# One fp32r pass less in fc1: w1 split into a power of two and a mantissa, with the scales multiplied into the sums in PSUM

## The reference, cut to what matters

```python
def _dequant(q, scales, g):                      # g = 128
    w = (q.astype(jnp.float32) - 128.0).reshape(K // g, g, N) * scales[:, None, :]
    return w.reshape(K, N)
pooled = ...                                     # scores, masked softmax, weighted sums, for each row
h = (pooled - mu) * rsqrt(var + EPS) * ln_gamma + ln_beta
w1 = _dequant(fc1_q, fc1_scales, 128)            # (512, 2048), scales (4, 2048)
y = silu(h @ w1 + fc1_bias)
w2 = _dequant(fc2_q, fc2_scales, 128)            # (2048, 512)
return x + pooled + 0.5 * (y @ w2 + fc2_bias)
```

## Time and profile before

| | us |
|---|---|
| time, median of three runs | 1589.35 (1588.07 to 1591.4) |
| the profiled execution: its time | 1588.93 |
| the profiled execution: its span | 1587.1 |

### The profile page before, as it was taken

One profiled execution on the slowest core, in us unless ns is written; L12 is line 12 of the kernel. 1 busy time (PEld: TensorE's weight loads), 2 busy tenths in 40 slices (PEclk: granted clock), 3 DMA queues, 4 the chain that ended last, 5 costly groups with the idle time before them and its releaser, 6 DMA issues.

```text
span 1587.1 us, 20994 instructions
## 1 busy us (share of the span) xinstructions
PE 1571.5 (99%) x7259; PEld 1270.1 (80%) x7259; DVE 950.5 (60%) x1918; ACT 432.0 (27%) x662; POOL 177.9 (11%) x156
## 2 busy tenths in 40 slices
PE   8999999999999999999999999999999999999999
PEld 5778788787887878788787887878878787887887
DVE  7887556655665565646666566556655656466522
ACT  3553322222231232312322222222322223123111
POOL 4102011110101101011110111101011010111100
PEclk9999999999999999999999999999999999999999
DMA  9803022040310404013040220403104040130200
GB/s 283 234 1 80 1 47 61 2 105 1 54 55 14 93 1 89 19 26 81 1 107 1 41 66 1 107 1 54 53 12 96 1 84 24 24 83 0 54 1 27
DMA packets 271311, 82.75 MB, mean 52 GB/s; under 512 B 247498, under 2 KB 248036, under 8 KB 270692
## 3 DMA queue, kind: packets, MB, share of 16 engines
q1 hardware_dynamic: 271152, 81.31, 21.7%
q10 hardware_dynamic: 52, 0.01, 0.0%
HBM read 49.83 MB, written 16.78 MB: 42 GB/s over the span
## 4 chain that ended last, share of the span: by engine, by line
PE 95%; DVE 3%; ACT 1%; issue 1%; DMA 0%; SPq 0%; DVEq 0%; ACTq 0%
PE y_ps L1045 14%; PE z_ps L1079 14%; PE z_ps L1080 14%; PE z_ps L1081 14%; PE y_ps L1046 14%; PE y_ps L1047 14%; PE a_ps L1009 1%; PE a_ps L1014 1%; PE a_ps L1010 1%; PE a_ps L1011 1%; PE a_ps L960 1%; PE a_ps L962 1%; PE a_ps L961 1%; PE a_ps L966 1%; PE a_ps L977 1%
## 5 line engine op out<-in xcount | busy, mean ns | idle before, releaser
L561 ACT ACTIVATE y_f<-y_ps,vec_cols 128x512 f32<-128x512 f32 x256 | 176.6, 690 | 912.7 <-PE y_ps L1047 901.8
L1045 PE MATMUL y_ps<-hT_hi,w_hi 128*128 128x512 f32 x1016 | 406.4, 400 | 0.3
L1079 PE MATMUL z_ps<-w_hi,y_hi 128*128 128x512 f32 x1024 | 398.7, 389 | 0.1
L1081 PE MATMUL z_ps<-w_hi,y_lo 128*128 128x512 f32 x1024 | 398.4, 389 | 0.0
L1080 PE MATMUL z_ps<-w_lo,y_hi 128*128 128x512 f32 x1024 | 398.4, 389 | 0.0
L1046 PE MATMUL y_ps<-hT_lo,w_hi 128*128 128x512 f32 x1016 | 396.7, 390 | 0.0
L1047 PE MATMUL y_ps<-hT_hi,w_lo 128*128 128x512 f32 x1016 | 396.6, 390 | 0.0
L849 DVE CAST y_hi<-y_f 128x512 fp32r<-128x512 f32 x240 | 109.6, 457 | 248.8 <-PE z_ps L1081 204.0
L1045 PEld LDWEIGHTS y_ps<-hT_hi,w_hi 128*128 128x128 f32 x1016 | 191.1, 188 | 60.2 <-issue 21.1
L1046 PEld LDWEIGHTS y_ps<-hT_lo,w_hi 128*128 128x128 f32 x1016 | 191.0, 188 | 42.1 <-issue 3.6
L1079 PEld LDWEIGHTS z_ps<-w_hi,y_hi 128*128 128x128 f32 x1024 | 192.2, 188 | 40.4 <-DVE w_lo L840 0.5
(11 more groups left out here) (208 smaller groups left out, 1199.8 us busy)
## 6 DMA issues: line engine op xcount, KB each, us to landing
x<-in_x_dram SPq DMA_DIRECT2D x64, 256.0 KB, 3.4
out_dram<-x SPq DMA_DIRECT2D x64, 256.0 KB, 2.2
x_cols<-in_x_dram SPq DMA_DIRECT2D x240, 64.0 KB, 2.2
h_cols<-scratch SPq DMA_DIRECT2D x224, 64.0 KB, 2.1
fc_codes<-in_L_ffn_fc_q_dram SPq DMA_DIRECT2D x8, 1024.0 KB, 15.2
fc_scaled<-in_L_ffn_fc_scales_dram SPq DMA_DIRECT2D x8, 1024.0 KB, 17.0
scratch<-in_L_cond_W_dram SPq DMA_DIRECT2D x1, 256.0 KB, 4.7
b2h<-in_L_ffn_fc_bias_dram SPq DMA_DIRECT2D x1, 256.0 KB, 15.4
```

Source lines behind the costliest of these rows:

```text
L561: nc.scalar.activation(y_f[k % 2][:], y_ps[k % 2][:], ACT.Silu, bias=b1[:, k:k + 1]).then_inc(silu_done, 1)
L1045: mm(o, w1_hi[:, c, cols], hT_hi[:, c, :], start=(c == 0), stop=False)
L1079: mm(z_ps[r][:], y_hi[k % 2][:, rows], w2_hi[:, k, :], start=(k == 0), stop=False)
L1081: last = mm(z_ps[r][:], y_lo[k % 2][:, rows], w2_hi[:, k, :], start=False, stop=(k == NF - 1))
```

## The change

w1 is kept as (code - 128) x 2^e, where e is the exponent of the scale. Such a value has at most 8 bits, so fp32r holds it exactly and there is no low part: `fc1` has two matmuls for each row block (w1 x hT_hi, w1 x hT_lo). The mantissas m of the scales, per output column, which is a PSUM partition, are applied to the sums. After row block c the sum is multiplied by m[c] / m[c + 1] (`ratio`), in place in PSUM, and Silu's own scale is m[3]. The multiplication (`rescale`) is ScalarE's for even k and VectorE's for odd k. TensorE's next matmul on that bank waits for it.

To give it time, fc1 works two k at a time, interleaved by c with fc2: an element is 32 slots, and slot i holds fc1(k, c), fc1(k + 1, c) with (k, c) from `fc1_slot(i)`, the conditioner's steps of that slot, and two of the four rows r of fc2(i // 2). So fc1 runs on into the next element from slot 27. The steps of the conditioner have new slots; those with a negative number are worked in slots 28 to 31 of the element before (in element 0 all are 4 later). `finish` is two and two, around slot 31's other steps. h is transposed into a buffer of its own, `h_rows`. SP loads the columns of x for element b + 1 ahead of `move_h(b)`. The exponential is in three pieces on three slots. The third and fourth load of w1's codes wait until the units of the first and second are made, since the scales' buffer is now double. The scales come in a second time, as 64 rows that TensorE transposes with the other vectors; RATIO makes mantissas and ratios of them in the prologue.

```diff
+        PE_PLAN = {-2: [("AT", 0)], -1: [("AT", 1)], 0: [("AT", 2)], 1: [("AT", 3)], 2: [("SC", 0)],
+                   9: [("USUM", 0), ("U", 0)], 11: [("DSUM", 0)], 13: [("PZ", 0)], 14: [("PZ", 1)], 15: [("PZ", 2)],
+                   16: [("PZ", 3)]}
+        ACT_PLAN = {-4: [("XT", 0)], -3: [("XT", 1)], -1: [("XT", 2)], 0: [("XT", 3)], 1: [("TANH", 0)], 2: [("SC", 0)],
+                    7: [("EXPE", 0), ("EXP", 0)], 8: [("EXP", 1)], 9: [("EXP", 2)], 10: [("U", 0)], 13: [("PZ", 0)],
+                    14: [("PZ", 1)], 15: [("PZ", 2)], 16: [("PZ", 3)]}
+        DVE_PLAN = {-4: [("TURN", 0), ("TURN", 1)], -3: [("XT", 0), ("TURN", 2)], -2: [("XT", 1), ("TURN", 3)],
+                    -1: [("XT", 2)], 0: [("XT", 3)], 1: [("PAR", 0)], 3: [("SCAN", 0)], 4: [("COLS", 0)],
+                    5: [("ROWMAX", 0)], 6: [("ARGS", 0)], 7: [("XS", 0)], 10: [("PC", 0), ("USUM", 0)],
+                    11: [("U", 0), ("XS", 1)], 12: [("DSUM", 0)], 14: [("LN", 0), ("XS", 2)],
+                    15: [("LN", 1), ("XS", 3)], 16: [("LN", 2)], 17: [("LN", 3)], 18: [("RSTD", 0)], 19: [("H", 0)]}
...
+        ACT_MOVED = {25: [("AFFINE", 0), ("AFFINE", 1)], 26: [("AFFINE", 2), ("AFFINE", 3)]}
+        DVE_MOVED = {24: [("TURNH", 0), ("TURNH", 1), ("TURNH", 2), ("TURNH", 3)], 26: [("SPLITH", 0), ("SPLITH", 1)],
+                     27: [("SPLITH", 2)], 28: [("SPLITH", 3)]}
...
+        DVE_LATE = {0: [("L2", 1), ("D1", 4)], 1: [("D2", 2)], 3: [("L2", 2)], 4: [("D2", 4)], 5: [("D1", 6)], 6: [("L2", 4)],
+                    8: [("D2", 6)], 9: [("D1", 8)], 10: [("L2", 6)], 12: [("D2", 8)], 13: [("D1", 10)], 14: [("L2", 8)],
+                    16: [("D2", 10)], 17: [("D1", 12)], 18: [("L2", 10)], 19: [("D2", 12)], 22: [("L2", 12)]}
...
+        def fc1_slot(i):
+
+            g, c = divmod(i + 5, ND)
+            return g // NH, 2 * (g % NH), c
...
+                for k0 in w1_unit:
+                    if k0 // NG == g - 2:
+                        sp.wait_ge(w1_unit[k0], 2)
                 load_w1(g)
                 load_w2(g)
...
             def turn(b, p):
 
+                sp.wait_ge(xs_used, (b + 1) * NJ)
+                load_columns(b + 1)
                 if not by_pe(b):
                     move_h(b)
-                sp.wait_ge(xs_used, (b + 1) * NJ)
-                load_columns(b + 1)
...
+            def rescale(b, k, c):
+
+                act.wait_ge(part_done, part_count(b, k, c))
+                nc.scalar.activation(y_ps[k % 2][:], y_ps[k % 2][:], ACT.Copy, scale=ratio[:, c * NF + k:c * NF + k + 1]).then_inc(scaled[0], 1)
...
+            def ffn(b):
+                for i in range(SLOTS):
+                    ahead, k, c = fc1_slot(i)
+                    if not (ahead and is_last(b)):
+                        if c < ND - 1:
+                            rescale(b + ahead, k, c)
+                        else:
+                            silu(b + ahead, k)
+                            silu(b + ahead, k + 1)
+                    if is_first(b) and i % 4 == 0:
+                        y_hi_part(i // 2 + 1)
+                    if is_first(b) and i % 4 == 3 and i < SLOTS - 1:
+                        y_hi_part((i + 1) // 2)
+                    for ahead, name, n in cond_steps(b, i, ACT_PLAN, ACT_TURN, ACT_MOVED):
+                        steps[name](b + ahead, n)
...
+            for c in range(3):
                 h_scaled(0, c)
+            act.wait_ge(ratio_ready, 1)
+            rescale(0, 0, 0)
+            h_scaled(0, 3)
+            for c in (1, 2):
+                rescale(0, 0, c)
+            for t in (0, 1):
+                silu(0, t)
+            y_hi_part(0)
+            for k0 in (0, 1):
+                w2_hi_part(k0)
+            rescale(0, 2, 0)
...
             def w1_values(k0):
+                q, e, w = w1_views(k0)
+                bits = e.bitcast(I32)
+                dve.wait_ge(w1_in[k0 // NG], 32)
+                v.tensor_scalar(bits, bits, 23, 23, ALU.logical_shift_right, ALU.logical_shift_left).then_inc(w1_unit[k0], 1)
+                dve.wait_ge(w1_unit[k0], 1)
+                v.scalar_tensor_tensor(w, q, -128.0, e, ALU.add, ALU.mult).then_inc(w1_unit[k0], 1)
...
+            def rescale(b, k, c):
+
+                dve.wait_ge(part_done, part_count(b, k, c))
+                v.tensor_scalar(y_ps[k % 2][:], y_ps[k % 2][:], ratio[:, c * NF + k:c * NF + k + 1], None, ALU.mult).then_inc(scaled[1], 1)
...
+            def ffn(b, p):
+                chains = {1: Chain(b + 1), 2: Chain(b + 2)}
+                for i in range(SLOTS):
+                    ahead, k, c = fc1_slot(i)
+                    if c < ND - 1 and not (ahead and is_last(b)):
+                        rescale(b + ahead, k + 1, c)
+                    if i % 4 == 0:
+                        split_y(b, i // 2 + 1)
+                    if i % 4 == 3 and i < SLOTS - 1:
+                        split_y(b, (i + 1) // 2)
+                    if i == SLOTS - 1:
+                        if not is_last(b):
+                            split_y(b + 1, 0)
+                        finish(b, p, 0)
+                        finish(b, p, 1)
+                    for ahead, name, n in cond_steps(b, i, DVE_PLAN, DVE_TURN, DVE_MOVED):
+                        steps[name](b + ahead, n, p if ahead == 2 else 1 - p, chains[ahead])
+                    if is_first(b):
+                        for name, k0 in DVE_LATE.get(i, []):
+                            weights[name](k0)
+                finish(b, p, 2)
+                finish(b, p, 3)
...
+            def fc1(b, k, c):
+
+                if c == 0:
+                    if k >= 2 or not is_first(b):
+                        pe.wait_ge(silu_done, b * NF + (k - 1))
+                    if is_first(b) and k in w1_unit:
+                        pe.wait_ge(w1_unit[k], 2)
+                else:
+                    pe.wait_ge(scaled[k % 2], scale_count(b, k, c - 1))
+                if k == 0:
+                    pe.wait_ge(hT_done, b * ND + (c + 1))
+                o, w = y_ps[k % 2][:], w1[:, c, k * P:(k + 1) * P]
+                mm(o, w, hT_hi[:, c, :], start=(c == 0), stop=False, skip_group_check=True)
+                last = mm(o, w, hT_lo[:, c, :], start=False, stop=True, skip_group_check=True)
+                last.then_inc(part_done if c < ND - 1 else fc1_done, 1)
...
+            def ffn(b, p):
+                for i in range(SLOTS):
+                    ahead, k, c = fc1_slot(i)
+                    if not (ahead and is_last(b)):
+                        fc1(b + ahead, k, c)
+                        fc1(b + ahead, k + 1, c)
+                    for ahead, name, n in cond_steps(b, i, PE_PLAN, PE_TURN, {}):
+                        steps[name](b + ahead, n, p if ahead == 2 else 1 - p)
+                    for r in (2 * (i % 2), 2 * (i % 2) + 1):
+                        fc2(b, i // 2, r)
```

More of the change, by code:

```diff
@@ L212, in build @@
         hT_done = sem("hT_done")
+        part_done = sem("part_done")
+        scaled = [sem(f"scaled{i}") for i in range(2)]
+        ratio_ready = sem("ratio_ready")
         fc1_done = sem("fc1_done")
@@ L228, in build @@
[L228 to L233, removed]
+        z_rows = sem("z_rows")
@@ L268, in by_pe, with cond_steps @@
             return isinstance(a, int) and a <= 1
-        def plan(b, early, steady):
-            return early if isinstance(b, int) and b == 0 else steady
+        def cond_steps(b, i, steps, turn, moved):
+            first = isinstance(b, int) and b == 0
+            out = []
+            if not (isinstance(b, int) and b == B - 1):
+                out += [(1, name, n) for name, n in steps.get(i - DELAY if first else i, []) if first or i >= 0]
+                out += [(1, name, n) for name, n in (turn if first else moved).get(i, [])]
+            if not (isinstance(b, int) and b >= B - 2):
+                out += [(2, name, n) for name, n in steps.get(i - SLOTS, [])]
+            return out
@@ L891, in _ @@
                     sum_identities()
+                elif name == "RATIO":
+                    scale_ratios()
                 else:
@@ L1071, in fc2 @@
-            def fc2(b, k):
-                if is_first(b) and k in w2_unit:
-                    pe.wait_ge(w2_unit[k], 3)
-                pe.wait_ge(split_done, b * NF + (k + 1))
-                if k == 0 and not is_first(b):
-                    pe.wait_ge(final_done, b * NJ)
-                for r in range(NJ):
-                    rows = slice(r * P, (r + 1) * P)
-                    mm(z_ps[r][:], y_hi[k % 2][:, rows], w2_hi[:, k, :], start=(k == 0), stop=False)
-                    mm(z_ps[r][:], y_hi[k % 2][:, rows], w2_lo[:, k, :], start=False, stop=False)
-                    last = mm(z_ps[r][:], y_lo[k % 2][:, rows], w2_hi[:, k, :], start=False, stop=(k == NF - 1))
-                    if is_last(b) and k == NF - 1:
-                        last.then_inc(last_rows, 1)
-                if not (is_last(b) and k == NF - 1):
-                    last.then_inc(fc2_done, 1)
```

(15 more changed lines are left out.)

286 lines of the change are left out of this document (110 added, 176 removed), and 7 rows, old and new, of tables (DVE_LATE, DVE_STEADY).

## The result

The changed kernel takes 1622.2 us against 1589.4: a ratio of 1.0197, 95% interval 1.0173 to 1.0222, so it is slower, though the interval doesn't say whether by more or by less than 2%. Ratio and interval rest on two runs, of 1622.2 and 1620.0 us; a third took 2727.1 us at the full clock, for a reason that nothing here shows. The forecast was 1580, faster. The profiled execution has a span of 1620.6 us, 33.5 more than before, at a mean granted clock of TensorE of 0.963, where before had 0.999.

The account below looks back on a forecast made before the run. TensorE, busy for 99% of the span, was taken as the bound. 1587.1 + 10.6 (element 0) + 13 x (96.5 - 96.6) - 4.5 (element 14) - 13.5 (element 15) = 1578.1, with 1.8 outside 1580 us; range 1530 to 1622.

Parts of the forecast that it names:

- What it takes away: In fc1, one of three matmuls goes: 1024 at 0.227 us, 232 us, leaving a period of 82.1 us.
- What it adds: 48 multiplications in PSUM per element, 24 on ScalarE at 0.69 us and 24 on VectorE at 0.75 us.
- rival 1: VectorE's multiplication in PSUM runs at SBUF's rate, 0.49 us, saving about 4 us an element: 1528 us; chance 0.15.
- The loop: In steady slots TensorE waits for multiplications queued behind other work: 14.4 us a period, making it 96.5 us.
- Slot 24's multiplication behind the transposes: On VectorE, rescale 25 queues behind h's transposes, which wait for move_h: TensorE waits 3.6 us.
- XT chain on ScalarE: Around slot 28, XT 0 waits for TURN 0 and ScalarE's rescale 29 stands behind it: 2.1 us.
- slot 31 and its neighbours: split_y, finish steps and XT 2 and 3 delay projections 2 and 3: waits of 1.1 and 0.6 us.
- the slack misses: In slots of 3 modulo 4, split_y precedes the next slot's fc2, leaving 0.09 us slack: 0.8 us added.
- Rival 2: Waits overlap as one long stall empties the queues, so they cost 8 us an element: 1496 us; chance 0.12.
- TensorE resumes 0.05 us after a VectorE end and loses 0.11 on the first matmul: At TensorE's restart after a wait for VectorE: 0.05 us to resume, 0.11 us lost on the first matmul.
- Element 0 and the start: Slot 0 starts at 52.5, 6.7 us later; VectorE's full queue makes element 0 end at 158.0, +10.6 us.
- Rival 3: GpSimd's adds block VectorE inside the loop, costing 2.3 us an element: 1612 us; chance 0.28.

Follow-up runs that it names:

- run 1: The changed kernel without any of the multiplications in PSUM and without the waits for them: 1390.2 us.
- Run 2: The changed kernel with idle matmuls added in elements 1 to 14, 12 in slot 26 and 7 in slot 30: 1580.9 us.
- run 7: The changed kernel with TensorE turning h in every element, without move_h's DMAs, multiplications still split over both engines: 1577.9 us.
- run 11: The kernel with all multiplications on ScalarE, TensorE held once per steady element until VectorE has made 8 chained copies: 1448.5 us.
- run 10: The kernel with all multiplications on ScalarE, TensorE held once per steady element until VectorE has made 6 chained copies: 1424.0 us.

## Why the prediction was wrong, by its own steps

- **What it takes away: right.** 1024 matmuls, 232 us. But "a period would be 82.1" was 1.5 too low: without any multiplication it is 83.6 (run 1), of which 1.0 is waits that the forecast hadn't.
- **What it adds: right.** 0.75 and 0.69 us were forecast, 0.753 and 0.660 measured; rival 1 (0.49) is refuted. The Silus with a column scale took 0.774 us against 0.69, which I had not priced; 16 of them an element, 1.3 us of ScalarE.
- **The loop: right in place and order, more than a third too dear.** Slot 24's multiplication behind the transposes 3.0 (forecast 3.6), XT chain on ScalarE 1.7 (2.1), slot 31 and its neighbours 1.2 in three waits (1.7), slots 3 and 4 1.35 and 1.64 (1.5 and 2.0), slot 19 0.3 (0.65), slot 15 1.0 (1.3); slots 5 to 7 nothing (0.8), and 0.3 for the slack misses (0.8). Together 10.5 for 14.4. I had priced each wait by hand from a slot that starts on time. Rival 2, in which only 8 us would be left, was closer than the forecast on this term.
- **The step that failed: "TensorE resumes 0.05 us after a VectorE end and loses 0.11 on the first matmul".** It took every matmul at 0.227 us whatever stood before it. Behind the waits of 3.0 and 1.65 us each of some 8 matmuls takes 0.43 (639.74 to 642.73): 2 x 8 x 0.2 = 3.2 us a period. 83.6 + 10.5 + 3.2 = 97.3; measured 98.9. 0.11 for each of ten restarts is 1.1 more, and 0.5 us stay unexplained; up to 1.5, as the 1.0 us of waits within the 83.6 may be among the 10.5 too. Run 2 shows the term: with the clock held up the kernel takes 1580.9 us, by chance the forecast to a microsecond, though that run's sum has too few waits and too low a floor in it.
- **Element 0 and the start: 7.3 us too low.** Slot 0's fc1 starts at 54.82 (forecast 52.5), and the element ends at 165.3 (158.0). In the prologue TensorE waits 3.6 us for the rows of vectors, of which 64 are now scales brought by DMA (before, it waited 2.7 us for x near there); in element 0 it waits 3.8 us for weights, and the clock is 0.94:

```profile
PE y_ps L990 <- DMA vec_rows<-in_L_ffn_fc_scales_dram: 3.6, 1, 3.6
PE y_ps L1111 <- DVE w L873: 3.8, 2, 2.7
...
54.82:165.30 110.48, 95.19 (x404) 72.24 (x405) 97.74 (x151) 57.88 (x87) 19.78 (x12) 0.94 0.29 81
```

  0.06 x 2 x 110.5 = 13 us at the half clock, some 6.6 lost by it. My sum by VectorE's queue (101 us of it, and 97.7 measured) was near; it was TensorE's side that I hadn't summed.
- **The whole miss:** 7.3, 31.3 in 13 periods of 2.4, and 3.9 in the last two elements: 42.5 us of span, 1620.6 for 1578.1. The clock's part in it, half of 120 - 3 us, is 58, more than the whole miss; the waits, priced too high, hid some of it.
- **Rival 3, GpSimd's blocking, gave a time close to the result (1612), for another reason than the one found.** The blocking is there: the low parts of xt at L733 take 1.031 and 0.896 us on the mean (before, at L691, 0.710 and 0.684). But TensorE's waits for them are 1.2 us a period, less than the 1.7 in my sum for slot 31 and after. In run 7 the same blocking did reach the loop. What it is worth in the changed kernel no run measures.
- **The range** ended at 1622.0, 0.2 us short, and only because rival 3 was in it. A rival of this sum's own kind was missing: "each long wait also costs the clock behind it". At two stretches a period it is 14 x 3.2 = 45 us, decides the sign, and could have been seen before: element 0 had a clock of 0.98 in the earlier trace rows beside the 2.02 us wait of the earlier trace rows, a steady element 1.00. The kernel before, right behind the matmul at 70.63 from which I took the 0.11 us (windows view, columns as in the earlier trace rows):

```profile
71.30:74.70 3.40, 3.40 (x9) 2.65 (x8) 3.40 (x3) 2.10 (x3) 3.40 (x3) 0.50 0.95 388
```

  Nine matmuls in 3.40 us, at the clock 0.50. I had read these rows up to 0.7 us ahead of it.

## What to carry to other kernels

Price a new wait of TensorE twice: its own length, and what follows at the lower clock; here waits of 1.65 to 3.0 us could cost another 1.5 to 1.7. When a step is put between two matmuls of one sum, ask first in which engine's queue it stands and what is the longest or longest-waiting thing ahead of it there: here the choice of engine was worth 211 us, from 1622 to 1411, and halving the instruction's duration, which I had taken most care over, 78. A share of busy time hides both: VectorE was busy for 74%, TensorE for 89% with part of it at half speed.

## What the chip did that I had not expected

- TensorE's granted clock fell to the half (1.2 of 2.4 GHz) after waits of 3.0 us and 1.65 us in one period of a kernel in which it was else nearly always busy, and after 8 of 14 nearly equal waits of 2.4 to 2.5 us in run 11; not after 14 waits of some 1.5 us in run 10. In the changed kernel all 14 waits of 2.96 to 3.95 us behind the transposes were followed by it, and all 12 of 1.65 us behind XT 0, but none of the 14 of 1.62 to 1.66 us behind COLS (at 582.20 in the period shown): the length alone doesn't decide. A stretch of 3.4 us cost 1.5 us in run 11, and 1.7 by the lost pulses.
- Matmuls whose result nobody reads, put where TensorE waits, can pay: 266 of them made the kernel 41 us faster.
- A multiplication of 512 columns in PSUM, in place, costs VectorE 0.753 us and ScalarE 0.660; of 128 columns VectorE 0.354.
- A Silu with its scale in a column took 0.774 us, the same without one 0.69.

- Beside GpSimd's adds a cast on VectorE took 1.14 us for 0.42, and a subtraction of two arrays 1.67 for 0.69 (run 7).

Left open: why in run 7 the half clock came after 10 of 13 waits of 2.27 to 2.33 us and not after the other three, what GpSimd's adds cost the changed kernel, and 0.5 to 1.5 us of the period.
